# Row maxima of an attention kernel turned by VectorE and laid by four small DMAs instead of TensorE and ScalarE

## The reference

```python
Q = split_heads(x @ Wq.T + bq); K = split_heads(x @ Wk.T + bk); V = split_heads(x @ Wv.T + bv)
tQ = split_heads(tokens @ Wq.T + bq); tK = split_heads(tokens @ Wk.T + bk)
scores = einsum('bhqd,bhkd->bhqk', Q + tQ, K + tK) / sqrt(32)
out = einsum('bhqk,bhkd->bhqd', softmax(scores), V)      # float32 throughout
return x + out
```

## Time and profile before

| | us |
|---|---|
| median of 3 runs | 761.67 (759.21 to 763.13) |
| the profiled execution's own time | 762.52 |
| its span, first to last instruction | 760.4 |
| TensorE busy | 722.4 (95%) |
| VectorE, ScalarE, GpSimd busy | 486.6, 453.8, 487.5 |
| mean granted TensorE clock | 0.980 of full speed |

### The profile page before, as it was taken

The page is one execution under the profiler, slowest core; times in us unless marked ns, Lnnn a source line. Parts: engine busy times, 40 slices in busy tenths (PEclk is TensorE's granted clock), DMA queues, the critical chain, the costliest instruction groups (busy, mean ns, idle before and its releaser), DMA issues.

```text
span 760.4 us, 10209 instructions
## 1 busy us (share of the span) xinstructions
PE 722.4 (95%) x3624; PEld 450.4 (59%) x3624; DVE 486.6 (64%) x757; ACT 453.8 (60%) x783; POOL 487.5 (64%) x206
## 2 busy tenths in 40 slices
PE   5869999999999999999999999999999999998876
PEld 2647666666666656666666666656566666664321
DVE  6265666766666666666666776665667666665635
ACT  4325666655666666556666666566666555665562
POOL 4223667776766677676667776666677766665770
PEclk9998999999999999999999999999999999999888
DMA  6984776666777766678776666687766667777101
GB/s 222 137 112 70 97 111 109 107 106 108 114 116 106 114 100 102 107 106 126 101 120 105 109 105 107 104 120 102 110 108 107 93 94 99 112 97 100 39 28 42
DMA packets 44210, 79.33 MB, mean 104 GB/s; under 512 B 5760, under 2 KB 5760, under 8 KB 44160
## 3 DMA queue, kind: packets, MB, share of 16 engines
q1 hardware_dynamic: 44160, 78.69, 65.6%
HBM read 19.95 MB, written 8.39 MB: 37 GB/s over the span
## 4 chain that ended last, share of the span: by engine, by line
PE 81%; DMA 8%; ACT 5%; DVE 3%; issue 2%; SPq 1%; ACTq 0%; DVEq 0%
PE bank L183 20%; PE bank L261 16%; PE bank L273 14%; PE bank L240 14%; PE bank L199 10%; DMA res<-xT 5%; PE bank L281 3%; ACT Qs L399 2%; ACT Pt L408 2%; PE bank L247 2%; DMA Ks<-lo 1%; SPq L658 1%; DMA xr<-xT 1%; ACT hi L384 1%; DVE mf L478 1%
## 5 line engine op out<-in xcount | busy, mean ns | idle before, releaser
L478 DVE TENSOR_REDUCE mf<-bank 128x1 f32<-128x512 f32 x512 | 345.4, 683 | 206.1 <-PE bank L240 204.9
L408 ACT ACTIVATE Pt<-bank 128x512 f32<-128x512 f32 x512 | 302.0, 599 | 241.6 <-PE bank L261 235.5
L604 POOL TENSOR_TENSOR A<-A,Pt 128x2048 f32<-128x2048 f32 x62 | 284.7, 4591 | 35.0 <-ACT Pt L408 34.8
L261 PE MATMUL bank<-Qs,Ks 128*128 128x512 f32 x512 | 223.6, 438 | 8.6 <-ACT Qs L399 6.6
L240 PE MATMUL bank<-Ks,Qs 96*128 96x512 f32 x512 | 206.5, 403 | 14.0 <-DVE mf L478 11.3
L604 POOL TENSOR_TENSOR A<-Pt 128x2048 f32<-128x2048 f32 x31 | 143.0, 4612 | 100.8 <-ACT Pt L408 100.8
L261 PEld LDWEIGHTS bank<-Qs,Ks 128*128 128x128 f32 x512 | 97.1, 190 | 119.7 <-issue 54.1
L273 PE MATMUL bank<-Pt,V 128*32 128x512 f32 x992 | 123.4, 616 | 0.9 <-DVE ot L515 0.9
L240 PEld LDWEIGHTS bank<-Ks,Qs 96*128 96x128 f32 x512 | 97.8, 191 | 32.8 <-DVE mf L478 18.2
L183 PE MATMUL bank<-Xh,Wh 128*128 128x512 f32 x256 | 102.8, 402 | 9.3 <-DVE Wl L453 9.3
L183 PE MATMUL bank<-Xh,Wl 128*128 128x512 f32 x256 | 102.5, 401 | 0.0
(11 more groups left out here) (56 smaller groups left out, 411.2 us busy)
## 6 DMA issues: line engine op xcount, KB each, us to landing
Qs<-hi SPq DMA_DIRECT2D x64, 256.0 KB, 5.6
Ks<-hi SPq DMA_DIRECT2D x64, 256.0 KB, 6.9
Qs<-lo SPq DMA_DIRECT2D x32, 256.0 KB, 7.1
Ks<-lo SPq DMA_DIRECT2D x32, 256.0 KB, 8.3
res<-xT SPq DMA_DIRECT2D x32, 256.0 KB, 8.2
outT<-ot SPq DMA_DIRECT2D x32, 256.0 KB, 2.0
xr<-xT SPq DMA_DIRECT2D x28, 256.0 KB, 2.8
Pt<-xT SPq DMA_DIRECT2D x4, 256.0 KB, 4.1
```

The lines of the kernel that those rows point to most:

```text
L261: e.matmul(STB[u % 2][:, :], Ks[:, sl, j, kc * P:(kc + 1) * P], Qs[:, sl, j, :], start=True, stop=True).then_inc(t_st, 1)
L408: e.activation(Pt[:, kc, j, :], STB[u % 2][:, :], ACT.Exp, scale=SCALE).then_inc(a_e, 1)
L478: e.reduce_max(mf[:, g % 2, m:m + 1], MXB[u % 2][:, :], AXX).then_inc(v_mx, 1)
L604: e.tensor_tensor(A[:, :, :], Pt[:, 0, :, :] if kc == 1 else A[:, :, :], Pt[:, kc, :, :], ALU.add).then_inc(p_a, 1)
```

## The change

The maxima now take two contraction rows instead of 32. GpSimd writes the 16 high parts and 16 low parts of a group side by side into `mx` (128 x 32), VectorE turns `mx` in 32x32 blocks (`maxima_turned`, after the row maximum of slot 11), and SP lays the four blocks of partitions into partitions 96 and 97 of `Qs` by four DMAs of 4 KB (`maxima_rows`, last in SP's list of a step). `row_maxima` writes its columns in the order head, query block. `Ks` holds -1 in partitions 96 and 97, and the scores matmul contracts over 98 rows instead of 128. `spread` and `spread_row` are gone, with the identity and its setup; the first scores matmul of a group waits for the four DMAs, the others for nothing new. `MAX_LEAD` becomes 7.

```diff
-MAX_LEAD = 5
+MAX_LEAD = 7
-LATE_VALUES, EARLY_VALUES, SPREAD = 5, 12, 14
-ROWS_AT = (14, 15, 16, 17)
+LATE_VALUES, EARLY_VALUES = 5, 12
+TURN_AT = 11
@@ tensor
-            def spread(g): ...            # four 128-column matmuls against ident, after slot 14
             def scores(g, n):
-                if kc == 0:
-                    e.wait_ge(a_bc, 4 * g + j + 1)
-                    if j == 0 and g < NSLOT:
+                if n == 0:
+                    e.wait_ge(d_mr[g % 2], 64 * (g // 2 + 1))
+                    if g < NSLOT:
                         e.wait_ge(p_ks, g + 1)
-                e.matmul(STB[u % 2][:, :], Ks[:, sl, j, kc * P:(kc + 1) * P], Qs[:, sl, j, :],
+                e.matmul(STB[u % 2][:, :], Ks[0:98, sl, j, kc * P:(kc + 1) * P], Qs[0:98, sl, j, :],
@@ scalar
-            def spread_row(g, j): ...     # PSUM -> Qs[96:128, g % 3, j, :], after slots 14, 15, 0, 1
@@ vector
+            def maxima_turned(g):
+                e.wait_ge(p_ml, g + 1)
+                if g >= 2:
+                    e.wait_ge(d_mr[g % 2], 64 * (g // 2))
+                e.transpose(mt[:, g % 2, :], mx[:, g % 2, :].bitcast(F32)).then_inc(v_mt, 1)
...
+                    if (g := due(t, n, TURN_AT, 1, 1)) is not None:
+                        maxima_turned(g)
@@ gpsimd
-                e.tensor_copy(mx[:, g % 2, 96:112], mf[:, g % 2, :]).then_inc(p_mh, 1)
+                e.tensor_copy(mx[:, g % 2, 0:16], mf[:, g % 2, :]).then_inc(p_mh, 1)
...
-            (identity and ef patterns, three copies of ef into Ks ahead of Wl)
+            for sl in range(NSLOT):       # behind the four subtractions of Wl
+                e.memset(Ks[96:98, sl, :, :].bitcast(F32), -1.0).then_inc(p_ks, 1)
@@ sync
+            def maxima_rows(g):
+                if g >= NSLOT:
+                    e.wait_ge(t_st, SLOTS * (g - NSLOT + 1))
+                e.wait_ge(v_mt, g + 1)
+                rows = Qs[96:98, g % NSLOT, :, :].rearrange("h j (q a i) -> h (j q) a i", a=4, i=32)
+                for a in range(4):
+                    e.dma_start(rows[:, :, a, :].bitcast(F32),
+                                mt[32 * a:32 * a + 32, g % 2, :]).then_inc(d_mr[g % 2], 16)
...
             stack(1, 2)
+            maxima_rows(0)
             for t in range(G):
...
                     store(t - 1)
+                if t + 1 < G:
+                    maxima_rows(t + 1)
```

More of the change, by code:

```diff
@@ L62, in cond_attention @@
         mf = sb("mf", [P, 2, 16])
-        mx = sb("mx", [P, 2, 144], F32R)
-        ident = sb("ident", [P, P], F32R)
-        idf = sb("idf", [P, P])
+        mx = sb("mx", [P, 2, 32], F32R)
+        mt = sb("mt", [P, 2, 32])
         ones = sb("ones", [P, HD])
-        ef = sb("ef", [P, 4])
         cT = sb("cT", [P, KC, 32])
@@ L85, in cond_attention @@
         d_st = [[sem(f"d_st{i}{qk}") for qk in range(2)] for i in range(NSLOT)]
+        d_mr = [sem(f"d_mr{i}") for i in range(2)]
         d_res = sem("d_res")
@@ L89, in cond_attention @@
         p_sel = sem("p_sel")
-        p_c = sem("p_c")
         p_ks = sem("p_ks")
@@ L102, in cond_attention @@
         a_v = sem("a_v")
-        a_bc = sem("a_bc")
         a_e = sem("a_e")
@@ L112, in cond_attention @@
         v_mx = sem("v_mx")
+        v_mt = sem("v_mt")
         v_f = sem("v_f")
@@ L119, in cond_attention @@
         t_mx = sem("t_mx")
-        t_mt = sem("t_mt")
         t_st = sem("t_st")
@@ L141, in freed @@
             return {"q": (v_lo, 2 * g + 1), "k": (v_lo, 2 * g + 2), "v": (a_v, g + 1),
-                    "mt": (a_bc, 4 * g + 4), "sum": (v_f, FIN * g + 1)}[kind]
+                    "sum": (v_f, FIN * g + 1)}[kind]
         def st_unit(g, kc, j):
@@ L212, in condition @@
                     e.wait_ge(d_c, 64)
-                    e.wait_ge(v_c, 4)
+                    e.wait_ge(v_c, 2)
                 for kc in range(KC):
@@ L241, in maxima @@
                          start=True, stop=True).then_inc(t_mx, 1)
[L243 to L249, removed]
             def scores(g, n):
@@ L328, in tensor_program @@
                 maxima(u)
-            spread(0)
             for t in range(G):
@@ L351, in tensor_program @@
                                 last_values(kc)
-                    if n == SPREAD and t + 1 < G:
-                        spread(t + 1)
             last_values(2)
@@ L392, in v_copy @@
                 e.activation(V[:, b % 2, c, :], ring_bank(("v", g))[:, :], ACT.Copy).then_inc(a_v, 1)
[L394 to L399, removed]
             def exps(g, n):
@@ L429, in scalar_program @@
             qk_hi(1, 2)
-            for j in range(4):
-                if ROWS_AT[j] < SLOTS:
-                    spread_row(0, j)
             for t in range(G):
@@ L436, in scalar_program @@
                     exps(t, n)
-                    for j in range(4):
-                        if (g := due(t, n, ROWS_AT[j], 1, 0 if ROWS_AT[j] >= SLOTS else 1)) is not None:
-                            spread_row(g, j)
                     if (g := due(t, n, V_AT, 3, 3)) is not None:
@@ L474, in row_maxima @@
                 g, m = divmod(u, SLOTS)
+                qc, j = divmod(m, 4)
                 if m == 0 and g >= 2:
@@ L477, in row_maxima @@
                 e.wait_ge(t_mx, u + 1)
-                e.reduce_max(mf[:, g % 2, m:m + 1], MXB[u % 2][:, :], AXX).then_inc(v_mx, 1)
+                e.reduce_max(mf[:, g % 2, 4 * j + qc:4 * j + qc + 1], MXB[u % 2][:, :], AXX).then_inc(v_mx, 1)
+            def maxima_turned(g):
[3 more added lines that the diff above has]
+                e.transpose(mt[:, g % 2, :], mx[:, g % 2, :].bitcast(F32)).then_inc(v_mt, 1)
             def sums_turned(g):
@@ L528, in vector_program @@
             e.memset(ones[:, :], 1.0).then_inc(v_c, 1)
-            e.memset(mx[:, :, :].bitcast(F32), 0.0).then_inc(v_c, 1)
-            e.wait_ge(p_c, 3)
-            e.tensor_copy(ident[:, :], idf[:, :]).then_inc(v_c, 1)
             for kc in range(KC):
@@ L550, in vector_program @@
                     qk_lo(1, 2)
+                if u == 19:
+                    maxima_turned(0)
             for t in range(G):
@@ L588, in parts @@
                 e.wait_ge(v_mx, SLOTS * (g + 1))
-                if g == 0:
-                    e.wait_ge(v_c, 4)
                 if g >= 2:
-                    e.wait_ge(t_mt, g - 1)
-                e.tensor_copy(mx[:, g % 2, 96:112], mf[:, g % 2, :]).then_inc(p_mh, 1)
+                    e.wait_ge(v_mt, g - 1)
+                e.tensor_copy(mx[:, g % 2, 0:16], mf[:, g % 2, :]).then_inc(p_mh, 1)
                 e.wait_ge(p_mh, g + 1)
-                e.tensor_tensor(mx[:, g % 2, 112:128], mf[:, g % 2, :], mx[:, g % 2, 96:112].bitcast(F32),
+                e.tensor_tensor(mx[:, g % 2, 16:32], mf[:, g % 2, :], mx[:, g % 2, 0:16].bitcast(F32),
                                 ALU.subtract).then_inc(p_ml, 1)
@@ L607, in pool_program @@
             e.memset(sel[:, :], 0.0).then_inc(p_sel, 1)
[L608 to L612, removed]
             for j in range(4):
@@ L616, in pool_program @@
                                 pattern=[[-1, B]], channel_multiplier=1).then_inc(p_sel, 1)
[L617 to L625, removed]
             for kc in range(KC):
@@ L629, in pool_program @@
                                 ALU.subtract).then_inc(p_w, 1)
+            e.wait_ge(p_w, KC)
+            for sl in range(NSLOT):
+                e.memset(Ks[96:98, sl, :, :].bitcast(F32), -1.0).then_inc(p_ks, 1)
+            e.wait_ge(p_ks, NSLOT)
             for kc in range(3):
```

## The result

The changed kernel takes 782.92 us (median of 4 runs, 780.53 to 783.26), the kernel before 760.44 beside it: ratio 1.027, 95% interval 1.0244 to 1.0296. It is slower by 22 us; the forecast was 777 us, with a range of 762 to 792. The profiled execution took 783.26 us.

A forecast was written before the change was run, and what follows sets the result against it. TensorE, busy 95% of the span, was taken to set the pace, with the stack's landing deciding after the change. Terms 13.8 (steps) + 4 (before the loop) - 3 (last steps) gave +15 us: 777 us, range 762 to 792.

The forecast's parts named there:

- The lead: MAX_LEAD 7 puts the first maxima matmul in slot 9, before its data land at 14.3 us: step 22.3 us.
- The term of the steps: The 28 steady steps at 22.3 us each: 624.4 against 610.6 us, +13.8 us.
- the new wait hides the late ones: Steps 1 to 28: TensorE's new wait for the stack hides the late steps, in which VectorE waited for the residual.
- The removed work: Per step, spread's four matmuls gone, worth 0.45 us, and ScalarE's copies for slots 0 to 3, worth 0.40 us.
- rival A: Keys' landing follows their issue, 1.4 us earlier, so no wait: step 20.8 us, about 736 us in all; chance 0.13.
- The turn: VectorE's transpose of the maxima behind slot 11's row maximum: taken as 0.25 us, between nothing and 0.69.
- The small DMAs: Four added per steady step, issued in 0.35 to 0.61 us each, landing in time for slot 0: zero cost.
- C: Rival: the four small DMAs are late in every step, 1.4 us of wait in slot 0, about 816 us; chance 0.07.
- Before the loop: Group 0's rows queue behind the keys' stack, first scores matmul moves from 59.59 to about 64.1: +4 us.
- GpSimd's fills: The memsets of Ks, moved into an idle stretch of GpSimd, cost zero.
- The last steps: Steps 29 to 31, without ScalarE's copies setting the pace of slots 0 to 3: -3 us, between -6 and +1.
- B: Rival, half of A: keys' low part lands 0.6 us earlier, step 21.7 us, about 761 us; chance 0.10.

The follow-up runs named there:

- Experiments 1: Changed kernel with MAX_LEAD 5 instead of 7, nothing else: 740.66 us, ratio 0.9715 to the kernel before.
- experiment 2: Kernel before with MAX_LEAD 7 instead of 5, nothing else: 794.48 us, ratio 1.043.
- experiments 3: Changed kernel, MAX_LEAD 7, without the transfer of the second copy of the keys' high part from group 3 on: 733.99 us (one run).
- experiment 4: Changed kernel with the keys' stack issued later, after SP waits for five matmuls of the step: 796.12 us (one run).
- experiment 5: Changed kernel with the residual's load issued behind the store instead of behind the keys' stack: 777.03 us, ratio 1.0178 to the kernel before.
- seventh experiment: Changed kernel with MAX_LEAD 5, the residual loaded behind the store, and group 0's maxima turned and laid before the last keys' stack: 726.35 us.
- experiment 6: Kernel before with GpSimd's three pattern copies into Ks moved behind its four subtractions of Wl: 760.5 us against 761.49, ratio 0.9978.
- experiment 9: Changed kernel with MAX_LEAD 5 and group 0's maxima laid before the last keys' stack, residual's load where the change has it: 731.2 us.

## Why the prediction was right, by its own steps

**The lead decides, and the data land as forecast.** Forecast: landing 14.3 us behind the queries' issue, unmoved by the keys' earlier issue, then 0.2 and 7.8. The keys' low part was issued 4.65 us behind the queries' instead of 6.01 and took 9.7 us instead of 8.3: 14.35 against 14.3. The idle time ahead of L240 is 1.27 us, forecast 1.3. Experiments 1 and 2 show that it is the lead, 3 that it is what is queued ahead, and 4 that it isn't the moment of issue.

**The term of the steps was too small:** +20.4 us for +13.8. The typical step is 22.38 for 22.3, which is 2.2 us in 28. The other 4.4 us are late steps (22.55 to 22.92, and one of 24.34). I had said that the new wait hides the late ones. It does hide those of the kernel before, in which TensorE waited for VectorE (up to 0.9 us) and VectorE for the residual: no such wait is left in the 28 steps. But it brings others: a step whose pace the landing sets has no slack, and each lateness of the landing goes through. The first maxima matmul started 14.4 to 14.5 us behind the queries' issue in most steps and 14.6 to 15.0 in the eight late ones, and with the residual's load moved (experiment 5) it was never later than 14.52. So the sum lacked a term: one landing, 14.3, stood for all 28. The wait was 1.16 to 1.55 us in 24 of 28 steps and 1.7 to 1.85 in four. Behind one of the four the clock fell, behind another, a longer one, it didn't:

```profile
344.14 0.47 PE L240 MATMUL bank<-Ks,Qs 96*128 96x512 f32 x1 [1.83 <-DMA Ks<-lo]
...
636.33 0.47 PE L240 MATMUL bank<-Ks,Qs 96*128 96x512 f32 x1 [1.72 <-DMA Ks<-lo]
```

```profile
638.00:640.00 2.00, 2.00 (x6) 1.52 (x6) 0.95 (x2) 1.10 (x2) 0.06 (x1) 0.50 0.35 131
```

The step of the wait at 636.33 is the one of 24.34, and another with a wait of 1.72 us that kept its clock took 22.83: the fall cost some 1.5 us beyond the wait.

**The removed work has the forecast worth.** Without the wait the step is 20.87 us (experiments 3 and 7) where rival A's sum had 20.8.

**The turn:** 0.20 us where I took 0.25 from the earlier trace rows:

```profile
L461 DVE STREAM_TRANSPOSE mt<-mx x32: 199/201/211, 54.7 to 750.9; 128x32 f32<-128x32 f32 x32
```

**The small DMAs** were in time. The four are issued from 415.01 to 417.67, one each 0.66 us, a little above the dear end of my range (0.61), and the scores of slot 0 start at 419.50 without waiting. So the last, issued at about 417.0, lands within 2.5 us, and C is refuted. By the rule of the Trainium skill cited for C ("DMA: Bandwidth & Descriptors", section on why a DMA increments its semaphore by 16) each would go over two engines. The trace agrees. The last of the four (all that moved in the first row's window, 418.0 to 418.7) is 34 packets, 32 of data and two more, where a store of 256 KB is 144, 128 of data and 16 more, which looks like one more for each engine; and the share of the 16 engines that it keeps busy, 0.15 in the second row, is that of two or three:

```profile
DMA packets 34, 0.00 MB, mean 6 GB/s; under 512 B 34, under 2 KB 34, under 8 KB 34
...
418.30:418.48 0.18, 0.18 (x2) 0.14 (x1) 0.18 (x1) 0.18 (x1) 0.18 (x1) 1.00 0.15 23
```

So what failed in C is its price and not its premise: I had taken 0.25 us for a piece, as for one of 2 KB, and all 32 pieces of 128 bytes passed in about 0.2 us.

**Before the loop:** forecast +4, measured +2.3 (step 1's stack at 82.21 for 79.90). Two things were in it. The first scores matmul did wait for the rows behind the keys' stack, to 61.99 instead of 59.59:

```profile
52.80 1.19 SPq L630 DMA_DIRECT2D Ks<-hi  x2
54.04 0.61 SPq L634 DMA_DIRECT2D Ks<-lo  x1
54.90 2.73 SPq L643 DMA_DIRECT2D Qs<-mt  x4
...
61.99 0.79 PE L253 MATMUL bank<-Qs,Ks 98*128 98x512 f32 x1 [5.41 <-DMA Qs<-mt]
```

But all of it stood 3.2 us earlier than I had put it, since the start got faster: with the pattern copies gone from GpSimd's first 10 us, VectorE's subtractions take 0.69 us (experiment 6 shows it in the kernel before). I had written that GpSimd's fills cost nothing because they lie in idle time; I had not looked at what they slowed. The Trainium skill ("SBUF — State Buffer", section on SBUF's two separate sides) says that VectorE with two inputs in SBUF and GpSimd, if its operation reads SBUF as these copies do, share a pair of ports as an exclusive lock. By that rule each subtraction would end just behind a copy. The trace agrees: by the timeline and the durations under experiment 6 the copies start at 3.25, 5.08 and 7.38 and end at 5.14, 7.43 and 9.73, and the subtractions end 0.53 to 0.54 us (of the 0.69 that one takes alone) behind them, at 5.67, 7.97 and 10.27.

The clock took part of it back. The windows show the low stretch: two of the kernel before (the second is its whole length), then the kernel after and the seventh experiment; the clock stands third from the end. The first of them is also what the prediction's "0.51" rests on, for which the earlier trace rows has no row:

```profile
59.60:64.40 4.80, 4.80 (x11) 3.79 (x12) 1.38 (x2) 2.80 (x5) 0.00 (x0) 0.51 1.06 165
```

```profile
54.10:64.35 10.25, 6.30 (x16) 5.05 (x17) 4.02 (x6) 4.66 (x8) 1.63 (x3) 0.50 0.75 118
```

```profile
50.30:67.40 17.10, 7.59 (x16) 5.11 (x17) 5.43 (x9) 2.71 (x5) 1.62 (x3) 0.50 0.46 68
```

```profile
51.50:61.70 10.20, 6.46 (x15) 5.17 (x16) 4.53 (x7) 3.00 (x5) 1.26 (x1) 0.50 0.72 102
```

While TensorE stood still for the rows, the low level went on: 17.1 us instead of 10.25.

**The last steps:** forecast -3, measured -1.7 (from the last stack of the 28 steps to the end 68.2 us for 69.9). Step 29 met a long wait, and behind it the clock was at its lower level for some 10 us, which I had not put in; the small DMAs cost one wait of 0.4 us there, where I had 1.7:

```profile
727.66 0.76 PE L240 MATMUL bank<-Ks,Qs 96*128 96x512 f32 x1 [4.86 <-DMA Ks<-lo]
```

**The sum:** 2.3 + 20.4 - 1.7 = 21.0 us of span, for 4 + 13.8 - 3 = 14.8. The mechanism was right; the size of the steps' term was off by 6.6 us. That the term of the start came out close is luck: the 3.2 us that I had not seen there stood against 1.5 us more than I had put in for the rest of it.

**The rivals.** A and B need the landing to come sooner when the keys are issued sooner. It didn't (14.35 for 14.3 at an issue 1.36 us earlier), and experiment 4 shows the same for a later issue. C: none of the 28 steps of the changed kernel waits for the small DMAs, and in experiment 9 such waits come to 5.6 us in all, not 39. What stays open is what lets the clock fall behind one wait of 1.72 us and not behind another of 1.83 (at 344.14), and why the tail of experiment 6 got slower.

## What to carry to other kernels

Before you let an engine run further ahead, find out when the data of the new first unit land, and what they queue behind: here an earlier issue was worth nothing, two slots of lead cost 42 us, and one transfer less (733.99 us, one run) gained no less than the shorter lead (740.66). A loop whose pace a landing sets passes every late landing on, so a forecast from the typical step is too low. And fills of an idle engine aren't free if they share something with an engine that isn't idle: look at the durations of its neighbours while they run.

## What the runs showed of the hardware that I had not expected

- Six transfers of 256 KB from SBUF to SBUF, into 32 partitions each, pass at 125 to 134 GB/s with the DMA engines full, about 2.05 us each, in the kernels before and after and in experiment 2; loads at the start run at more than that (232 GB/s in the first of the page's 40 slices).

```profile
404.50:408.00 3.50, 3.50 (x25) 1.89 (x18) 1.22 (x2) 0.88 (x2) 1.26 (x1) 1.00 1.09 129
```

- A load of 256 KB issued 0.6 us behind the last transfer of the stack delayed its landing by 0.1 us in the typical step and by up to about 0.5 in some (experiment 5).
- Behind waits of 1.6 to 1.9 us in a TensorE that otherwise hardly waits, the clock fell to its lower level for about 3.4 us in some steps, eight of 28 in experiment 4 and one of 28 in the kernel after; in other steps of both it didn't, behind waits of up to 1.84 us.
- A DMA of 4 KB in 32 pieces of 128 bytes was 34 packets, which passed in about 0.2 us; the packets of the last of four were through 1.5 us behind its issue.
- A VectorE subtraction of 128x512 took 2.37 us instead of 0.69 beside a GpSimd copy of 32x2048, and the copy 2.35 instead of 1.89.
